# A wait in the middle of every batch of gathers, in a graph layer with attention and experts

## What is computed

```python
xn = layernorm(x)
msgs = xn[src] * edge_weight[:, None]
agg = segment_sum(msgs, dst, num_segments=6250)
x = x + agg @ gnn_weight + linear_attention(xn)    # 8 heads of 64, k and v normalized per head
y = layernorm(x)
# top 2 of 16 experts: relu(y @ w1[e] + b1[e]) @ w2[e] + b2[e], weighted by a softmax
x = x + layernorm(y + moe(y))
```

## Time and profile before

| what | before |
|---|---|
| median of three runs | 1520.85 us (1519.32 to 1523.46) |
| span of the profiled execution | 2053.1 us |
| PE busy in it | 1168.8 us, 57% |
| POOL busy in it | 1005.6 us, 49% |
| DVE and ACT busy in it | 651.8 and 406.3 us |
| mean granted TensorE clock | 0.780 |

### The profile page before, as it was taken

The page is one execution under the profiler, slowest core; times in us unless marked ns, Lnnn a source line. Parts: engine busy times, 40 slices in busy tenths (PEclk is TensorE's granted clock), DMA queues, the critical chain, the costliest instruction groups (busy, mean ns, idle before and its releaser), DMA issues. The chain is left out here.

```text
span 2053.1 us, 23292 instructions
## 1 busy us (share of the span) xinstructions
PE 1168.8 (57%) x6546; PEld 848.9 (41%) x6546; DVE 651.8 (32%) x2406; ACT 406.3 (20%) x1093; POOL 1005.6 (49%) x1094
## 2 busy tenths in 40 slices
PE   0278888976423767432576324773266367576681
PEld 0144444544313655221554213552154156465670
DVE  7144344333632212223112131122212222412568
ACT  4033232321101312000211001210021022222221
POOL 2746666664365244566254663446624643204634
PEclk9899999987755888655788666887577588887885
DMA  9345444432134656233574325653364274366784
GB/s 329 97 151 185 154 153 155 141 90 62 47 98 153 217 187 216 80 91 117 176 238 143 90 92 183 196 178 90 121 220 162 85 265 143 124 210 217 244 256 138
DMA packets 155049, 323.09 MB, mean 157 GB/s; under 512 B 24769, under 2 KB 97729, under 8 KB 154785
## 3 DMA queue, kind: packets, MB, share of 16 engines
q1 hardware_dynamic: 65760, 148.16, 21.9%
q0 software_dynamic: 49296, 134.68, 21.6%
q10 hardware_dynamic: 39856, 38.67, 5.6%
HBM read 257.06 MB, written 64.36 MB: 157 GB/s over the span
## 5 line engine op out<-in xcount | busy, mean ns | idle before, releaser
L855 POOL DMA_INDIRECT ring<-normed_rows,src_sb x831 | 797.9, 960 | 780.0 <-PE ps L1512 462.2
L1661 PE MATMUL ps<-room 128*128 128x256 f32 x952 | 270.5, 435 | 115.9 <-issue 79.9
L1648 PE MATMUL ps<-room 128*128 128x128 f32 x1904 | 279.8, 300 | 70.3 <-issue 58.6
L1648 PEld LDWEIGHTS ps<-room 128*128 128x128 f32 x1904 | 260.4, 214 | 80.0 <-issue 75.2
L1661 PEld LDWEIGHTS ps<-room 128*128 128x128 f32 x952 | 199.8, 221 | 155.4 <-issue 85.3
L1445 DVE TENSOR_TENSOR desk<-ps,room 128x256 f32<-128x256 f32 x121 | 51.3, 424 | 587.6 <-PE ps L1661 293.4
L1512 PE MATMUL ps<-ring,S 128*32 128x256 f32 x1680 | 145.6, 453 | 153.0 <-DVE aggT L1116 77.9
L1539 PE MATMUL ps<-room,tT 128*128 128x512 f32 x392 | 196.7, 644 | 11.4 <-issue 11.1
L967 ACT ACTIVATE room<-ps,room 128x128 f32<-128x128 f32 x476 | 136.1, 369 | 303.5 <-remote 201.2
L846 POOL DMA_INDIRECT ring<-results_by_slot,slot_i x98 | 96.5, 984 | 146.4 <-issue 80.9
L1512 PEld LDWEIGHTS ps<-ring,S 128*32 128x32 f32 x1680 | 60.8, 125 | 211.8 <-issue 188.4
(11 more groups left out here) (226 smaller groups left out, 1247.0 us busy)
## 6 DMA issues: line engine op xcount, KB each, us to landing
room<-in_w2b SPq DMA_DIRECT2D x92, 640.0 KB
room<-in_w1b SPq DMA_DIRECT2D x92, 514.0 KB
room<-rows_by_slot SPq DMA_DIRECT2D x121, 128.0 KB
results_by_slot<-desk ACTq DMA_DIRECT2D x121, 128.0 KB
rows_by_slot<-desk ACTq DMA_DIRECT2D x6, 2432.0 KB
ring<-normed_rows,src_sb POOLq DMA_INDIRECT x831
normed_rows<-X SPq DMA_DIRECT2D x7, 896.0 KB, 8.0
result<-ring SPq DMA_DIRECT2D x49, 128.0 KB
```

What stands on the lines that cost most here:

```text
L855: pool.indirect_dma_start(out=ring[:, b % 2 * BT + m, :], out_offset=None, in_=table, in_offset=bass.IndirectOffsetOnAxis(ap=src_sb[:, b * ...
L1648: mm = pe.matmul(hps[g % 2][:, f * TS:(f + 1) * TS], w1_sb[g % WB][:, k * F + f * P:k * F + (f + 1) * P], xgT[g % 2][:, k, :], start=(k == ...
L1661: mm = pe.matmul(ops, hT[g % 2][:, f, :], w2_sb[g % WB][:, f * D:(f + 1) * D], start=(f == 0), stop=(f == FC - 1))
```

## The change

POOL waits behind the sixth gather of a batch (m = 5) until the batch's first six gathers have signalled that they have landed, and issues the other six then. The last batch has three gathers and so no such wait.

```diff
                         in_offset=bass.IndirectOffsetOnAxis(ap=src_sb[:, b * BT + m:b * BT + m + 1], axis=0),
                     ).then_inc(gathered[b % 2], 16)
+                    if m == BT // 2 - 1:
+                        pool.wait_ge(gathered[b % 2], 16 * (BT * (b // 2) + BT // 2))
                 for stage in POOL_AFTER[b]:
                     {"scatter": scatter, "pick": pick}[stage[0]](stage[1])
```

## The result

The changed kernel takes 1688.84 us (median of four, 1685.67 to 1694.23) against 1522.15 of the kernel before on the same chip: a ratio of 1.108, interval 1.1045 to 1.112, or 166.7 us more. (Ratios and intervals come from all the runs and can differ by 0.2% from the ratio of two medians.) The forecast was 1633 in a range of 1585 to 1683. The direction was right and the growth of 112.5 us too small by a third, so that the measured time lies 6 us above the range.

What follows compares the result with a forecast made beforehand. The prediction took POOL's back-to-back issuing of gathers to pace the runs. Pauses 103.5 us, plus 24 for landings under load, less 15 hidden, gave 112.5; 1520.85 + 112.5 = 1633 us, range 1585 to 1683.

Steps and rivals of the forecast that it cites:

- The runs are paced by POOL with a few seams: Before the tail, POOL issues back to back for 95% of roughly 1250 us, with 40 to 60 us of waiting.
- 69 pauses, each a real wait: In 69 of the 70 batches the added wait's count is reached only when all six gathers have landed.
- 1.5 us net for a pause with nothing else in flight: Gap ahead of the seventh gather grows from 0.3 to 1.8 us; 69 x 1.5 = 103.5 us, bounds 1.25 and 2.0 each.
- PE's 1.97 in the earlier trace: PE's first edge block starts 1.97 us behind batch 0's last gather; source of the pause's upper bound of 2.0.
- 24 us for landings under load: Eight pauses meet a zero fill of the experts' rows or a results fill, 3 us more each; bounds 0 and 80.
- The bound of 80: Upper bound for pauses meeting fills: ten pauses at 8 us each.
- 15 us hidden: Ten pauses covered where POOL waits for PE anyway, at slots 19, 25 and 26: -15 us; bounds 0 and -30.
- Hidden wholly: Rival, chance 0.05: PE paces at 23.8 us a batch, pauses only take from POOL's waits; price 0, time 1521.
- Hidden in the first stage: Rival, chance 0.15: PE holds batches 3 to 20 at 16.5 to 18 us, hiding 18 pauses; time 1597.
- The clock: Rival, chance 0.12: PE's clock falls in added idle time, some 35 expert batches add 1.2 us each; time 1675.
- Slow landings everywhere: Rival, chance 0.10: 2.0 us net in each pause plus half the fills' bound, 178 us; time 1699.
- The span would grow by 0 to 60 us: Profiled span grows much less than the runs, since pauses and stops overlap there.

Runs made afterwards that it cites:

- pair without weight loads: Kernel before and changed kernel, both without the experts' weight loads after the first three tiles: 1480.51 us and 1609.78 us (ratios to before 0.9702 and 1.0551).
- early batches: Kernel before with the pause behind the sixth gather in batches 0 to 24 alone: 1569.24 us against 1525.02, ratio 1.0292.
- late batches: Kernel before with the pause behind the sixth gather in batches 25 to 68 alone: 1646.34 us, ratio 1.078.
- twice: Changed kernel with two pauses a batch, behind the fourth and the eighth gather, 138 in place of 69: 1840.9 us, ratio 1.2066 to the kernel before.
- at the end: Changed kernel with the pause moved from behind the sixth gather to behind the twelfth: 1685.57 us, ratio 1.1052 to the kernel before.
- second profile: The kernel before, unchanged, profiled again: span 1520.3 us, of a run of 1522.14 us.

## Why the prediction was right in its mechanism and wrong in size

One rule accounts for all the kernels: gaps of the pauses, less 0.3 us each, less what POOL's waits for PE fell from 43.2 (from 23.1 in the pair without weight loads). The last two columns are the difference of the medians and that of the two profiled spans.

| pause | gaps, less 0.3 each | less fall of the waits for PE | sum | medians | spans |
|---|---|---|---|---|---|
| the change | 214.2 - 20.7 = 193.5 | 43.2 - 12.7 = 30.5 | 163.0 | 166.7 | 163.6 |
| early batches | 61.1 - 7.5 = 53.6 | 43.2 - 34.0 = 9.2 | 44.4 | 44.2 | 47.1 |
| late batches | 159.9 - 13.2 = 146.7 | 43.2 - 20.5 = 22.7 | 124.0 | 121.3 | 133.6 |
| twice | 393.7 - 41.4 = 352.3 | 43.2 - 4.8 = 38.4 | 313.9 | 315.9 | 320.4 |
| at the end | 215.1 - 20.4 = 194.7 | 43.2 - 12.2 = 31.0 | 163.7 | 160.5 | 163.1 |
| no weight loads | 159.0 - 20.7 = 138.3 | 23.1 - 11.4 = 11.7 | 126.6 | 129.3 | 127.1 |

The rule is an account of POOL's time: it comes out when the gathers' own durations and the tail stay as they were. It misses the most for the late pauses, whose profile is of the slowest of their four runs (1655.72 us). There the gathers and scatters took 3.5 us more and the tail 3.6. (Its 159.9 us are 157.8 in 43 places and 2.1 in the 44th, which the profile puts down to ACT.) What speaks for the theory beyond the account is that it was stated before the other five ran. It came within 2 us for the early and the late pauses and inside its range for the end. For two pauses a batch it was 24 us too high, and without the weight loads 19 us too low.

- **The runs are paced by POOL with a few seams.** Right. The sum of POOL's work and the tail left 40 to 60 us of waiting by the prediction (1520.85 less its own terms gives 33 to 53, since its sum was 4 us over the median); 43.2 were there, and the tail was 268.0 us, inside its 265 to 285. The places were named wrongly for the most part: the longest wait, 16.3 us ahead of batch 25, comes from the mixing and routing of slot 22, and the mid stage of slot 19 and the expert tiles of slots 25 and 26 have only the 1.9 and 7.0 us ahead of batches 22 and 29. Of the stops in the first profile the second has none that shows. What caused them isn't settled; no run here tells it.
- **69 pauses, each a real wait.** Right: 69 rows of 69.
- **1.5 us net for a pause with nothing else in flight.** Too low. The gap was 2.06 instead of 1.8, so 1.76 net and 121 us for 69, not 103.5. The last bytes were as read from the earlier trace rows. What I missed comes behind them: I took the 0.3 us of a release by PE, but POOL starts about 0.6 us after the last bytes of a gather. PE's 1.97 in the earlier trace rows, which I had kept as a bound, was the nearer row.
- **24 us for landings under load.** This is the step that failed: "Eight zero fills of the experts' rows ... I count 8 pauses that meet one, at 3 us more each". I loaded the pauses with the zero fills alone and left out the expert weights. What the gaps cost over 121 us is 193.5 - 121 = 72. Of this, 55 go with the weight loads, as the pair without them showed. Of the other 17, the zero fills have 10: only four pauses stood in or right behind one, not eight, in batches 4, 7, 12 and 15, with gaps of 5.1, 5.9, 3.8 and 3.7 us. The 7 left stand from batch 25 on. The second of the four, with the fill that ACT issued just before it:

```profile
183.36 0.54 ACTq L886 DMA_DIRECT2D rows_by_slot<-desk  x1
...
190.68 0.94 POOL L855 DMA_INDIRECT ring<-normed_rows,src_sb  x1 [5.92 <-DMA ring<-normed_rows,src_sb]
```

So the term for the fills alone was too large (24 for 10), and the one for the weights was at nothing (for 55). The bound of 80 held the 72, but for the wrong transfers, and my own range took only 24 of it together with the 2.0 us of each pause. "If the gaps are 3 us and more (landing sized wrongly)" was my sign of being wrong, and the mean gap was 3.1.

- **15 us hidden.** 30.5 were, at the edge of my bounds (0 to 30). It partly made up for the others.
- **The rivals.** Hidden wholly: no, though a reader of the first profile's 462.2 us of waiting for PE would have said so. Hidden in the first stage: no, as the early pauses alone show. The clock: the granted share fell from 0.865 to 0.837, but POOL's waits for PE fell too, so PE never held a batch that it had not held before, and the mean of the tiles' last products was 385 ns against 386 in the second profile of before. Slow landings everywhere (1699) came nearest in size. It is not what happened: the quiet pauses were at 2.0 to 2.2 us, and most of the rest sat in those with expert tiles.
- **The span would grow by 0 to 60 us.** Wrong: it shrank by 369, as the first profile's stops were absent from the second.

The sum with the measured terms: 121 + 72 - 30.5 = 163, against 163.6 by the two undisturbed spans. How the weight loads hold up a gather's landing, in the DMA engines or in the memory, no run here tells.

No version beat the kernel before. The experiments point only at taking the pause out, or at waiting for what has already landed, which is no gain.

## What to carry to other kernels

Here POOL issued transfers back to back and set the pace, and a wait in it for its own newest transfer cost the rest of that transfer's way each time, some 1.8 us with little else in flight; the same wait for transfers 7.5 us older was free. Look for this wherever one queue paces a kernel. Price such a wait by the landing time beside the loads that the same stretch really has in flight, taken from the windows' DMA share, and not by one isolated transfer. And when a profile's span is far from the runs' times, add up the work of the suspected bound first: here that sum was right where the waits of the profile pointed the other way.

## What I had not expected of the hardware

- One profiled execution of an unchanged kernel spanned 2053.1 us and another 1520.3, with runs at 1519 to 1534. In the long one PE, ACT and DVE stood still together for up to 15 us at a time, with no transfer issued by SP in most of these stretches, while POOL issued its gathers at the usual pitch until it had to wait for PE. The second profile has only one such stretch of over 3 us in the gathering, ahead of batch 0's products. One of them, 9.5 us long (busy us of PE, PEld, DVE, ACT and POOL, then granted clock, DMA share, GB/s):

```profile
1155.50:1165.00 9.50, 0.00 (x0) 0.00 (x0) 0.00 (x0) 0.00 (x0) 7.28 (x8) 0.65 0.37 104
```

- The bytes of a 128 KB gather are through 1.25 to 1.5 us behind the end of its record when the DMA engines are otherwise nearly free. With their share at 0.99 (365 GB/s) the gap until POOL went on was 5.7 us, and it grew to 6.1 elsewhere in the changed kernel, though hardly more than gathers were in flight in the row above, at 104 GB/s.
- From the last bytes of a gather to POOL's next gather it took about 0.6 us, and 0.3 from the end of PE's products. The difference doesn't lie in POOL: the trace has the semaphore's signal 0.26 us ahead of POOL's start in both cases, so the signal comes about 0.3 us after the last bytes and almost at once behind PE's products.
